# The pair streams of a layer-norm pipeline: the one tile per group that VectorE normalised is normalised by GpSimd

## The reference

```python
def _ln(x, w):
    m = jnp.mean(x, axis=-1, keepdims=True)
    v = jnp.mean((x - m) ** 2, axis=-1, keepdims=True)
    return (x - m) * jax.lax.rsqrt(v + EPS) * w
...
pp = _ln(protein_pair, ln_w)          # (1, 256, 256, 128)
cp = _ln(compound_pair, ln_w)         # (1, 64, 64, 128)
...
pp = jax.nn.sigmoid(pp @ gw2) * (pp @ w2 + b2)
cp = jax.nn.sigmoid(cp @ gw1) * (cp @ w1 + b1)
...
block1 = jnp.einsum('bikc,bkjc->bijc', pp, ab1)
block2 = jnp.einsum('bikc,bjkc->bijc', ab2, cp)
```

## Time and profile before

| what | value |
|---|---|
| median of 3 runs (lowest, highest) | 2257.28 us (2257.18, 2268.9) |
| span of the profiled execution | 2257.4 us |
| busy, share of the span: PE, DVE, ACT, POOL | 78%, 65%, 56%, 53% |
| compound_sums' groups in the span | about 130 to 176 us |
| protein_sums' groups in the span | about 204 to 492 us, its last products until 508 us |

### The profile page before, as it was taken

One profiled execution on the slowest core, in us unless ns is written; L12 is line 12 of the kernel. 1 busy time (PEld: TensorE's weight loads), 2 busy tenths in 40 slices (PEclk: granted clock), 3 DMA queues, 4 the chain that ended last, 5 costly groups with the idle time before them and its releaser, 6 DMA issues. The chain is left out here.

```text
span 2257.4 us, 48343 instructions
## 1 busy us (share of the span) xinstructions
PE 1756.7 (78%) x11055; PEld 1507.4 (67%) x11055; DVE 1461.8 (65%) x6046; ACT 1255.3 (56%) x3198; POOL 1186.0 (53%) x1844
## 2 busy tenths in 40 slices
PE   6967798885755540899999997477866579999995
PEld 5957688883534340899999997355864357878884
DVE  6965898976875640444444443698338977777776
ACT  5765989964543310565665664344446656665554
POOL 5855777740677776355555556688546520002220
PEclk9988999995555555999999999688986779999998
DMA  4021444422222153222222220784862100000004
GB/s 155 0 76 49 123 122 121 119 70 67 84 76 76 53 154 69 82 78 75 76 76 75 74 78 29 221 225 116 142 128 61 51 1 0 0 0 0 0 0 150
DMA packets 247581, 177.99 MB, mean 79 GB/s; under 512 B 93415, under 2 KB 213541, under 8 KB 247468
## 3 DMA queue, kind: packets, MB, share of 16 engines
q1 hardware_dynamic: 230060, 142.71, 23.6%
q0 software_dynamic: 17408, 34.00, 4.5%
HBM read 123.76 MB, written 54.97 MB: 79 GB/s over the span
## 5 line engine op out<-in xcount | busy, mean ns | idle before, releaser
L1597 POOL DMA_INDIRECT choices<-y,small x288 | 286.1, 993 | 225.4 <-ACT y L1627 155.2
L1279 POOL DMA_INDIRECT sorted_tokens<-work x256 | 249.6, 975 | 138.0 <-issue 77.4
L1660 PEld LDWEIGHTS banks<-w,hidden 128*128 128x128 f32 x2304 | 268.1, 192 | 5.5
L1660 PE MATMUL banks<-w,hidden 128*128 128x128 f32 x2304 | 268.5, 275 | 0.0
L1710 PEld LDWEIGHTS banks<-small 128*128 128x128 f32 x1536 | 192.8, 191 | 62.7 <-issue 32.4
L1710 PE MATMUL banks<-small 128*128 128x128 f32 x1536 | 225.2, 283 | 12.1 <-ACT small L1744 8.6
L1791 POOL COPY work_again<-small 128x128 f32 x128 | 38.4, 300 | 349.8 <-DVE small L1774 349.8
L388 PE MATMUL banks<-ident,small 128*128 128x128 f32 x640 | 120.3, 306 | 120.2 <-ACT small L375 74.3
L1701 PE MATMUL banks<-ab_tiles,small 128*128 (+1 forms) x768 | 210.0, 383 | 1.1 <-DVE small L1974 1.1
L1627 ACT ACTIVATE y<-y,small 128x128 f32<-128x128 f32 x288 | 92.3, 391 | 196.3 <-DVE y L1568 196.3
L375 ACT ACTIVATE small<-small 128x128 f32<-128x128 f32 x384 | 161.7, 484 | 34.5 <-POOL small L352 33.9
(11 more groups left out here) (267 smaller groups left out, 4536.6 us busy)
## 6 DMA issues: line engine op xcount, KB each, us to landing
small<-L_conv_protein_pair SPq DMA_DIRECT2D x128, 256.0 KB
rows<-sorted_tokens SPq DMA_DIRECT2D x72, 262.0 KB, 2.9
ab_tiles<-choices SPq DMA_DIRECT2D x32, 512.0 KB, 3.9
work_again<-L_conv_protein_pair SPq DMA_DIRECT2D x32, 512.0 KB, 7.5
x_tiles<-x SPq DMA_DIRECT2D x32, 256.0 KB, 3.7
work<-x SPq DMA_DIRECT2D x32, 256.0 KB, 2.9
after_mixture<-x_tiles SPq DMA_DIRECT2D x32, 256.0 KB, 2.2
work_again<-after_mixture SPq DMA_DIRECT2D x32, 256.0 KB, 2.7
```

What stands on the lines that cost most here:

```text
L1279: pool.indirect_dma_start(out=self.sorted, out_offset=bass.IndirectOffsetOnAxis(ap=where[:, u // BATCH, u % BATCH * G + t, k:k + 1], axis= ...
L1597: pool.indirect_dma_start(out=self.out, out_offset=bass.IndirectOffsetOnAxis(ap=where[:, u, t:t + 1], axis=0), in_=y[:, u % 4, t, :], in_o ...
L1660: last = pe.matmul(out[:, t * P:(t + 1) * P], hidden[:, u % 2, h, t * P:(t + 1) * P], w2[:, u % 2, h * P:(h + 1) * P], start=h == 0 and t ...
```

## The change

Tile 0 moves from DVE to POOL. DVE's step `apply` is gone from its list, and POOL gets `apply_pool` at the end of its step for the group, after the power and the shift. PE's transposes wait for the new semaphore `applied_pool` where they waited for `applied`. ACT's three tiles, the loads, the buffers and all other steps stay. It holds for both uses of PairStream, so 16 + 128 instructions move.

```diff
@@ class Norm
+        self.pool_tiles, self.by_dve = pool_tiles, G - by_act - pool_tiles
+        if pool_tiles:
+            self.applied_pool = Flow(chip, "applied_pool", depth)
...
-        for t in range(G - self.by_act):
+        for t in range(self.by_dve):
             last = dve.tensor_scalar(self.zn[:, u, t, :], src[:, t, :], self.mv[:, u, t, 0:1],
                                      self.r[:, u, t:t + 1], ALU.subtract, ALU.mult)
         self.applied.done(last)
+
+    def apply_pool(self, pool, src, n, u):
+        self.scaled.ready(pool, n)
+        self.turned.free(pool, n)
+        pool.sem_inc(self.paced, 1)
+        for t in range(self.by_dve, self.by_dve + self.pool_tiles):
+            last = pool.tensor_scalar(self.zn[:, u, t, :], src[:, t, :], self.mv[:, u, t, 0:1],
+                                      self.r[:, u, t:t + 1], ALU.subtract, ALU.mult)
+        self.applied_pool.done(last)
...
-        if self.by_act < G:
+        if self.by_dve:
             self.applied.ready(pe, n)
+        if self.pool_tiles:
+            self.applied_pool.ready(pe, n)
@@ class PairStream
-        self.norm = Norm(chip, carve, (EPS_LN,), banks=(0, 1), depth=4, zn=self.stage, by_act=3, by_pool=True)
+        self.norm = Norm(chip, carve, (EPS_LN,), banks=(0, 1), depth=4, zn=self.stage, by_act=3, by_pool=True,
+                         pool_tiles=1)
...
-    def apply(self, dve, n, u):
-        self.norm.apply(dve, self.stage[:, u, :, :], n, u)
+    def scale(self, pool, n, u):
+        self.norm.rstd(pool, n, u)
+        self.norm.apply_pool(pool, self.stage[:, u, :, :], n, u)
@@ compound_sums, protein_sums
-                    engine_loop(pool, groups, 4, [(lambda n, u: stream.norm.rstd(pool, n, u), 0)])
+                    stream.norm.open_pool_tiles(pool)
+                    engine_loop(pool, groups, 4, [(lambda n, u: stream.scale(pool, n, u), 0)])
...
-                            [(lambda n, u: stream.stats(dve, n, u), 0), (lambda n, u: stream.apply(dve, n, u), 1),
-                             (gate, 4), (add_blocks, ADD_LAG)],
+                            [(lambda n, u: stream.stats(dve, n, u), 0), (gate, 4), (add_blocks, ADD_LAG)],
                             peel=quarters * per_chunk)
```

More of the change, by code:

```diff
@@ L274, with __init__ @@
 class Norm:
-    def __init__(self, chip, carve, eps, banks, depth=2, zn=None, width=E, by_act=0, by_pool=False, by_root=False):
+    def __init__(self, chip, carve, eps, banks, depth=2, zn=None, width=E, by_act=0, by_pool=False, by_root=False,
+                 pool_tiles=0):
         self.by_act, self.by_pool, self.by_root = by_act, by_pool, by_root
+        self.pool_tiles, self.by_dve = pool_tiles, G - by_act - pool_tiles
+        if pool_tiles:
+            self.applied_pool = Flow(chip, "applied_pool", depth)
         if by_root:
@@ L307, in open_pe, with open_pool_tiles @@
         self.turned.open(pe)
+    def open_pool_tiles(self, pool):
+        self.applied_pool.open(pool)
     def open_act(self, act):
@@ L734, in gate @@
                         stream.gate(dve, cp[:, bass.ds(n * G, G), :], n, u)
-                    engine_loop(dve, groups, 4, [(lambda n, u: stream.stats(dve, n, u), 0),
-                                                 (lambda n, u: stream.apply(dve, n, u), 1), (gate, 4)])
+                    engine_loop(dve, groups, 4, [(lambda n, u: stream.stats(dve, n, u), 0), (gate, 4)])
                 for c8 in range(C // 8):
@@ L889, in _ @@
                     stream.norm.open_pool(pool)
-                    engine_loop(pool, quarters * per_chunk, 4, [(lambda n, u: stream.norm.rstd(pool, n, u), 0)])
+                    stream.norm.open_pool_tiles(pool)
+                    engine_loop(pool, quarters * per_chunk, 4, [(lambda n, u: stream.scale(pool, n, u), 0)])
             @block.vector
```

## The result

| | before | after |
|---|---|---|
| median | 2263.09 us (4 runs, 2257.18 to 2270.97) | 2297.16 us (4 runs, 2295.9 to 2299.65) |
| span of the profiled execution | 2257.4 us | 2294.7 us |
| pace in protein_sums, groups 4 to 127 | 2.180 us | 2.448 us |

After takes 1.0154 times as long, 95% interval 1.0121 to 1.0186: slower, and above the forecast's range (2246 to 2268).

A forecast was written before the change was run, and what follows sets the result against it. A buffer's round was taken to bound the early groups, the round and DVE nearly tied the later ones. Later gain 4.3 us, early loss 0.3 us: 2257.4 - 4.0 = 2253.4 us, range 2246 to 2268.

The forecast's parts named there:

- X: Duration of the moved tile's instruction on POOL: taken as 0.38 us, between 0.30 and 0.46, far bound 0.66.
- POOL gets the tile: Part on POOL's four steps of 1.65 us: with the tile added, POOL's pace becomes 1.98 us, 1.90 to 2.06.
- The first rival: POOL's tile delays the next group's first step, so POOL becomes the limit and the kernel slower; chance 0.22.
- its signs: In the later profile: POOL without idle time, and ACT waiting longer for POOL's shift.
- the forecast's own formula: POOL's pace is 1.65 + X - 0.05; its excess over 2.18 is paid 122 times on top of 2257.4 us.
- the term X - 0.05: What the tile adds to POOL's pace, 0.33 us, with the next step starting 0.05 us before the shift's end.
- a buffer's round: protein_sums, statistics to next statistics in one of four buffers: 8.34 us, 2.085 a group at best; limit early, near-tied later.
- The later stretch's gain: protein_sums groups 36 to 127: pace from 2.197 to 2.150 us a group, 4.3 us over 91 groups.
- DVE's freed slot: DVE without its tile saves 0.24 us a group; its pace goes from 2.11 to 1.87 us on average.
- the tile is hidden behind ACT's three: PE's transposes: POOL's tile ends before ACT's third tile, with 0.9 us to spare.
- taking the tile from DVE leaves the round as it is: PE's transposes wait for ACT last, so moving DVE's tile does not shorten the way through a buffer.
- compound_sums: Its 16 groups: DVE's freed time goes into waits for loads, 0 us; -2 us if half came through.

The follow-up runs named there:

- e1: Kernel before, with a list of POOL instructions of several kinds and widths added behind protein_sums' last group to price them; 2286.84 us in one run.
- e7: Kernel after, but POOL normalises 64 columns of tile 0 and DVE the other 64; 2273.87 us, ratio 1.0037 to before.
- e3: Kernel after, with the numbers 0 and 1 in place of the two columns in POOL's tile; 2280.43 us, ratio 1.0101 to before.
- e2: Kernel after without the tile on POOL, PE not waiting for it, tile 0 not normalised; 2256.93 us, ratio 0.9998 to before.
- e9: Kernel before, but in protein_sums a load waits for the transposes three groups back instead of four, so three buffers; 2337.64 us in one run.
- e8: Kernel after, but DVE adds eps and negates the mean, leaving POOL the power, shift and whole tile; 2262.74 us, ratio 1.0005 to before.
- e5: Kernel after, but POOL normalises tile 0 only in every second group, DVE in the others; 2267.57 us, ratio 1.0008 to before.

## Why the prediction was wrong

**The step that failed** is the upper bound of X, in the part "POOL gets the tile": the two-input add "reads twice as much as the tile does", so its 0.46 us was set above the tile, X was taken as 0.38, and POOL's pace as 1.98. The row was read rightly: a two-input multiply of 128x128 takes 0.454 us on POOL (e1). What failed is that a TENSOR_SCALAR must then be cheaper. It is another kind of instruction with its own price, 0.53 us with one operation and one number, 0.79 with two operations and two columns (e1), and 0.806 in its place, which makes POOL's round 2.45 and POOL the limit of the stage. The bounds came from rows of other operations, and the span between them said nothing of this one. A warning stood in the earlier trace rows: L346, a TENSOR_SCALAR of four elements with one input, takes 228 ns where the two-input add of four takes 199. It was read for its size only, not for its sign.

The Trainium skill's "GPSIMD Engine Reference", sections 3 and 8, with DVE about twice as fast, had given X near 0.63, the better guess of the two. Here the ratio is 0.806 us to the 0.31 of the earlier trace rows, 2.6. The Trainium skill's "GPSIMD Engine Reference", section 4.1, says that operations with one input run at roughly line rate on GpSimd and those with two inputs about twice as slow as on VectorE. In e1 the order is the other way round, and the measurement decides here: 0.528 us for a TENSOR_SCALAR with one input and one number, 0.454 for the TENSOR_TENSOR multiply of two inputs.

**The rest of the working.** The first rival, POOL becomes the limit, is what happened, with its signs: no wait of POOL for DVE, ACT waiting for the shift. Its points were too mild. It had the gain cancelled at X = 0.58 and 0.5% lost at 0.67; at 0.59 (e7, where DVE kept half a tile) the time was 0.4% above before and the pace 0.09 us above 2.18, some 11 us, and at 0.66 (e3) the pace was 0.10 above, some 12 us or 0.5%, and the time 1.0%. Put into the forecast's own formula, X = 0.806 gives a pace of 1.65 + 0.76 = 2.41 and 2257.4 + 122 x 0.23 = 2285. Of the 9 us that lack to 2294.7, half are the term X - 0.05: the overlap of 0.05 us between neighbours on POOL, read in the earlier trace rows, is hardly gained a second time; the tile adds 2.45 - 1.65 = 0.80 to the round, so 123 x 0.04 = 5 us. The other half lies outside groups 4 to 127, where part of it may be the spread of one execution against another.

That a buffer's round is the limit behind the engines fits e2 and e9, with the reservation made there. The later stretch's gain was sized at 0.047 us a group, and e2, with no tile at all, has 0.03. DVE's freed slot was sized rightly as well: it is what e8 spends. That the tile is hidden behind ACT's three was right (342.50 against 343.00). That taking the tile from DVE leaves the round as it is, because the transposes wait for ACT last, was not quite right. In groups 36 to 127 of before PE also waited for DVE's tile (us in total, times, longest):

```profile
PEld banks L388 <- DVE small L367: 10.1, 13, 1.3
```

For compound_sums the forecast had 0; at most the 1.7 us by which protein_sums' first group starts later can be its cost, and e1 and e9 differ by more than that at the same place.

So the change traded a slot of 0.24 us on an engine at 2.11 against 0.80 us on one at 1.65, with a limit near 2.15 for both; by that, some 0.50 us would have been free, an estimate that no run had in just that form (e8's round, 0.48 above 1.65, cost nothing, e7's, 0.59 above it, cost 0.4%).

## What to carry to other kernels

An operation is priced by an instruction of the same opcode, operand kinds and width on the same engine; if the trace has none, rows of other opcodes do not bound it, and the range has to reach well beyond them (here 0.46 was called the upper end, and 0.81 came). What a slot on the next engine may cost is the limit behind the engines (here a buffer's way over the number of buffers) less that engine's time without waits: 2.15 - 1.65 = 0.50 us here, as an estimate. Once the tile was there, taking 0.3 us of small steps off POOL undid the loss as well as taking the tile away did.

## What the runs showed of the hardware that was not expected

Half a tile on POOL costs 73% of a whole one (0.59 against 0.81 us): 0.37 us do not depend on its width.

The products behind the last group of protein_sums ran at either clock level in profiled executions whose stage before had run at the same granted clock, 1.00. The windows of the kernel before, and then of e5 (us, busy us of PE, PEld, DVE, ACT, POOL; granted clock, DMA):

```profile
480.00:490.00 10.00, 7.30 (x58) 6.45 (x56) 7.71 (x35) 8.67 (x22) 5.50 (x14) 1.00 0.15 44
...
500.00:510.00 10.00, 6.90 (x62) 6.73 (x61) 3.93 (x9) 0.74 (x1) 0.91 (x7) 1.00 0.01 2
```

```profile
480.00:490.00 10.00, 6.81 (x54) 5.92 (x52) 7.88 (x38) 8.37 (x22) 8.11 (x19) 1.00 0.18 52
...
500.00:510.00 10.00, 10.00 (x48) 10.00 (x48) 2.08 (x3) 0.00 (x0) 0.00 (x0) 0.50 0.01 2
```

In e5 the clock is at 0.50 (1.2 GHz) where before had 1.00 (2.4 GHz), and PE gets through 48 products at full occupation where before did 62 in 6.9 us. GpSimd's first instruction of the next phase marks the end of it:

```profile
508.94 0.78 POOL L1262 IOTA work<- 128x8 f32 x5 [21.77 <-POOLq L130]
```

```profile
521.45 0.66 POOL L1294 IOTA work<- 128x8 f32 x5 [31.82 <-POOLq L130]
```

That is 24.4 us after the last statistics in the one (484.5) and 35.8 in the other (485.7): 11 us at one place, over three times what the tile at no price gained in e2. From 480 to 490 us PE had been busy 7.30 and 6.81 of the 10 us, and in the next 10, in which e5's clock fell, 8.84 and 8.53; so its busy time ahead of the fall does not tell the two apart. What does stays open; no run was made on it.
